# Eight experts' weights held on chip and addressed by a register, in two expert blocks of an eight-block network

## The reference

```
# block index 3
flat = (x - mean) * rsqrt(var + 1e-5) * ln_scale + ln_bias
h_shared = swiglu(flat @ shared_in_w.T);  out_shared = h_shared @ shared_out_w.T + shared_out_b
h_expert = swiglu(flat @ expert_in_w.T)                       # 512 wide, the same for all experts
routed = cnt @ expert_out_bias + sum_e comb[:, e] * (h_expert @ expert_out_weight[e].T)   # two e per token
# block index 7
h = relu(xf @ W1[e] + b1[e]);  y = h @ W2[e] + b2[e]          # 256 -> 256 -> 256, e = 0..7
y = (y - mean(y)) / sqrt(var(y) + 1e-5) * gamma[e] + beta[e]
out = sum over the token's two experts of gate * y
```

## Time and profile before

| | us |
|---|---|
| three timed runs | 3156.28, 3156.52 (median), 3159.9 |
| the profiled execution's own time | 3158.89 |
| its span, first to last instruction | 3157.1 |
| norm, block 3 (1090.3 to 1101.3) | 11.0 |
| parameter wait and second norm (to 1115.3) | 14.0 |
| routing (to 1136.8) | 21.5 |
| plan (to 1159.6) | 22.8 |
| gated layers `srh` (to 1249.9) | 90.3 |
| shared and routed output `sro` (to 1381.2) | 131.3 |
| norm, block 7 (2965.3 to 2977.1) | 11.8 |
| routing (to 2996.6) | 19.5 |
| plan (to 3020.4) | 23.8 |
| experts `nee` (to about 3143) | 122.4 |

### The profile page before, as it was taken

How to read it: one execution, slowest core, us unless ns; L and a number is a source line. 1 busy time by engine, 2 the same in 40 slices (tenths; PEclk the granted TensorE clock), 3 DMA queues, 4 the chain that set the end, 5 groups by cost and what they waited for, 6 DMA issues and landing times. The chain is left out here.

```text
span 3157.1 us, 52623 instructions
## 1 busy us (share of the span) xinstructions
PE 2438.4 (77%) x18539; PEld 2039.5 (65%) x18539; DVE 1574.7 (50%) x3095; ACT 1142.8 (36%) x2211; POOL 553.1 (18%) x862
## 2 busy tenths in 40 slices
PE   6979599679957758855785999998989999844255
PEld 4858499579936634644784777777777777734153
DVE  3646412222236631143445677777677777732355
ACT  2333122012213211122213666656566656614421
POOL 0000122122212100420001111212112211120044
PEclk8999699789969969976897999999999999967587
DMA  4000022134231102720565231324244452021075
GB/s 124 1 7 1 26 84 90 63 96 143 75 96 64 35 27 87 243 81 22 220 266 155 74 105 35 91 87 130 66 136 128 115 142 64 18 57 38 8 230 190
DMA packets 147048, 293.48 MB, mean 93 GB/s; under 512 B 37154, under 2 KB 74056, under 8 KB 143716
## 3 DMA queue, kind: packets, MB, share of 16 engines
q1 hardware_dynamic: 127988, 237.43, 24.3%
q0 software_dynamic: 18800, 52.69, 6.1%
HBM read 488.56 MB, written 65.74 MB: 176 GB/s over the span
## 5 line engine op out<-in xcount | busy, mean ns | idle before, releaser
L2224 PE MATMUL tx_ring<-g_ident,tx_p 128*128 128x128 f32 x2552 | 394.6, 283 | 74.1 <-DVE tx_p_t L2464 35.8
L2224 PEld LDWEIGHTS tx_ring<-g_ident,tx_p 128*128 128x128 f32 x2552 | 286.2, 141 | 176.8 <-DVE tx_p_t L2464 58.6
L2464 DVE COPY tx_p_t<-tx_ring 128x512 f32<-128x512 f32 x464 | 305.6, 685 | 132.3 <-PE tx_ring L2224 129.7
L2457 DVE TENSOR_REDUCE tx_neg_max<-tx_scores 128x1 f32<-128x1354 f32 x232 | 362.0, 1561 | 16.1 <-PE tx_scores L2212 16.1
L2354 ACT ACTIVATE tx_p<-tx_scores,tx_neg_max 128x1354 f32<-128x1354 f32 x232 | 322.9, 1392 | 87.3 <-DVE tx_neg_max L2457 84.7
L2361 ACT ACTIVATE tx_p_t<-tx_ring 128x384 f32<-128x384 f32 x232 | 113.7, 490 | 294.8 <-PE tx_ring L2224 290.9
L2212 PE MATMUL tx_scores<-tx_keys,tx_queries 96*128 96x512 f32 (+1 forms) x696 | 202.2, 399 | 16.3 <-DMA tx_queries<-tx_q_hi 11.2
L2264 PE MATMUL tx_ring<-tx_p_t,tx_values 128*32 128x128 f32 x5104 | 174.2, 298 | 14.7 <-ACT tx_p_t L2361 12.8
L2264 PEld LDWEIGHTS tx_ring<-tx_p_t,tx_values 128*32 128x32 f32 x5104 | 156.3, 121 | 28.2 <-ACT tx_p_t L2361 24.0
L192 PE MATMUL ln_turned<-g_ident,g_xn 128*128 128x128 f32 x176 | 39.5, 409 | 138.3 <-DVE g_xn L179 138.3
L2212 PEld LDWEIGHTS tx_scores<-tx_keys,tx_queries 96*128 96x128 f32 x696 | 115.3, 193 | 27.5 <-issue 17.1
(11 more groups left out here) (910 smaller groups left out, 5265.2 us busy)
## 6 DMA issues: line engine op xcount, KB each, us to landing
tx_keys<-expert_keys SPq DMA_DIRECT2D x696, 169.5 KB
lv1e_w<-in_L_ffn_W SPq DMA_DIRECT2D x232, 256.0 KB
tx_w<-in_L_ffn_W SPq DMA_DIRECT2D x58, 1024.0 KB
lv0e_w<-in_L_ffn_W SPq DMA_DIRECT2D x200, 256.0 KB
tx_values<-expert_values SPq DMA_DIRECT2D x58, 704.0 KB
tx_rows<-in_L_ffn_rows SPq DMA_DIRECT2D x29, 640.0 KB, 3.7
sro_we<-_L_ffn_expert_out_weight SPq DMA_DIRECT2D x29, 512.0 KB, 5.5
nee_w<-in_L_ffn_w SPq DMA_DIRECT2D x58, 256.0 KB, 4.1
```

What stands on the lines that cost most here:

```text
L2224: last = nc.tensor.transpose(ring[u % 2][:, (t - t0) * P:(t - t0 + 1) * P], p[n % 2][:, t * P:(t + 1) * P], g.ident[:])
L2457: nc.vector.tensor_reduce(neg_max[:, n % 4:n % 4 + 1], sc[n % 2][:, 0:N], AX_X, ALU.max, negate=True)\
L2464: nc.vector.tensor_copy(p_t[:, n % TURNED, t0:t0 + nt, :], ring[u % 2][:, 0:nt * P].rearrange("p (t q) -> p t q", q=P))\
```

## The change

Both blocks get a class that owns all of the block's weights for its whole length: `RoutedWeights` (8 expert matrices of 512 KB, two of 1 MB, one of 512 KB, the gates, their bias and the norm's parameters: 14 DMAs, 6.8 MB) and `NormedWeights` (`w1`, `w2`, the two broadcast rows of each expert, 256 KB each, and its bias columns, 1 KB, with the gate: 33 DMAs, 6.3 MB). SP issues them all in the block's first stage, the norm. The stages after it load no weights any more. For each tile the engines that use the weights now read the owner themselves (`owners`) and put the register into the operand's address: PE in `sro`; PE, ACT and DVE in `nee`. The stationary `w1` of `nee` isn't addressed that way: ACT copies the tile's `w1` (128x512) into one of two buffers `w1_now` (`bring`), and PE waits for it.

```diff
-def stage_route(nc, g, tag, src_t, gate, width, rule, weights, mask, bias=None, keys=None):
+def stage_route(nc, g, tag, src_t, gate, width, rule, weights, mask, keys=None, held=None):
 
     with ExitStack() as ctx:
         s = Pool(nc, ctx, tag)
-        w = s.sb("w", [P, KD, width])
+        w, w_loaded, bias_all = held or (s.sb("w", [P, KD, width]), s.sem("w_loaded"), None)
...
+            if held is None:
+                sync.dma_start(w[:], gate.rearrange("(k p) e -> p k e", p=P)).then_inc(w_loaded, 16)
...
-def stage_gated_hidden(nc, g, tag, src_t, shared_dram, expert_dram, h):
+def stage_gated_hidden(nc, g, tag, src_t, held, h):
...
-            for i, dram in enumerate((shared_dram, expert_dram)):
-                sync.dma_start(w[i][:], dram.rearrange("(k p) o -> p k o", p=P)).then_inc(w_loaded[i], 16)
...
         def _(sync):
-            owner = {}
-
-            def expert(i):
-                if i not in owner:
-                    owner[i] = nc.sync.value_load(plan.owner[0:1, i:i + 1], min_val=0, max_val=plan.experts - 1)
-                return owner[i]
-
-            def load(i):
-                k = i % ROUTED_SETS
-                new = dict(cond=expert(i) != expert(i - ROUTED_SETS)) if i >= ROUTED_SETS else {}
-                sync.dma_start(we[:, k, :, :].rearrange("p k o -> p (k o)"),
-                               expert_dram[bass.ds(expert(i), 1)].rearrange("o p n -> p (o n)"), **new).then_inc(we_loaded[k], 16)
-
-            sync.dma_start(ws[:], shared_dram.rearrange("(k p) o -> p k o", p=P)).then_inc(ws_loaded, 16)
-            for i in range(ROUTED_SETS):
-                load(i)
             back.load_table(sync)
-            for i in range(ROUTED_SETS, tiles):
-                sync.wait_ge(done, i - ROUTED_SETS + 1)
-                load(i)
             back.load(sync, sent, all_sent)
...
+            of = owners(nc.tensor, plan)
...
-                pe.wait_ge(we_loaded[i % ROUTED_SETS], 16 * (i // ROUTED_SETS + 1))
+                if i == 0:
+                    pe.wait_ge(we_loaded, 16 * plan.experts)
...
-                    last = nc.tensor.matmul(row[i % 2][:, 0:D], hg_t[:, i % 2, f, :], we[:, i % ROUTED_SETS, f, :],
+                    last = nc.tensor.matmul(row[i % 2][:, 0:D], hg_t[:, i % 2, f, :], we[:, of(i), f, :].rearrange("p o n -> p (o n)"),
...
+    def load(self, sync):
+        a = self.a
+        sync.dma_start(self.affine[:], a["L1_ffn_affine"]).then_inc(self.affine_loaded, 16)
+        sync.dma_start(self.gates[:], a["L1_ffn_gates"].rearrange("(k p) e -> p k e", p=P)).then_inc(self.gates_loaded, 16)
+        sync.dma_start(self.gate_bias[:], a["L1_ffn_gate_bias"].partition_broadcast(P)).then_inc(self.gates_loaded, 16)
+        for i, name in enumerate(("L1_ffn_shared_in_w", "L1_ffn_expert_in_w")):
+            sync.dma_start(self.w_in[i][:], a[name].rearrange("(k p) o -> p k o", p=P)).then_inc(self.w_in_loaded[i], 16)
+        sync.dma_start(self.ws[:], a["L1_ffn_shared_out_w"].rearrange("(k p) o -> p k o", p=P)).then_inc(self.ws_loaded, 16)
+        for e in range(self.experts):
+            sync.dma_start(self.we[:, e, :, :].rearrange("p k o -> p (k o)"), a["L1_ffn_expert_out_weight"][e])\
+                .then_inc(self.we_loaded, 16)
...
-                    sync.dma_start(affine[:], a["L1_ffn_affine"]).then_inc(loaded, 16)
-                    sync.wait_ge(loaded, 16)
+                    sync.wait_ge(held.affine_loaded, 16)
...
+def owners(eng, plan):
+
+    held = {}
+
+    def of(i):
+        if i not in held:
+            held[i] = eng.value_load(plan.owner[0:1, i:i + 1], min_val=0, max_val=plan.experts - 1)
+        return bass.ds(held[i], 1)
+    return of
...
+    def load(self, sync):
+        a = self.a
+        sync.dma_start(self.gate[:], a["L3_ffn_Wg"].rearrange("(k p) e -> p k e", p=P)).then_inc(self.gate_loaded, 16)
+        for e in range(self.experts):
+            sync.dma_start(self.w1[:, e, :, :].rearrange("p k o -> p (k o)"), a["L3_ffn_w"][e, :, 0:KD * D])\
+                .then_inc(self.w_loaded, 16)
+            sync.dma_start(self.w2[:, e, :, :].rearrange("p k o -> p (k o)"), a["L3_ffn_w"][e, :, KD * D:2 * KD * D])\
+                .then_inc(self.w_loaded, 16)
+            sync.dma_start(self.b1[:, e, :], a["L3_ffn_cols"][e]).then_inc(self.small_loaded, 16)
+            sync.dma_start(self.rows[:, e, :, :].rearrange("p r d -> p (r d)"),
+                           a["L3_ffn_rows"][e:e + 1].rearrange("o r d -> o (r d)").to_broadcast([P, 2 * D]))\
+                .then_inc(self.small_loaded, 16)
...
+        w1_now = s.sb("w1_now", [P, 2, KD, D])
...
-            for i in range(SETS):
-                load(i)
             back.load_table(sync)
-            for i in range(SETS, tiles):
-                sync.wait_ge(second_done, i - SETS + 1)
-                sync.wait_ge(out_done, i - SETS + 1)
-                load(i)
...
-                pe.wait_ge(w_loaded[i % SETS], 32 * (i // SETS + 1))
+                pe.wait_ge(brought, i + 1)
...
-                    last = nc.tensor.matmul(row[i % 2][:, 0:D], h[:, i % 2, f, :], w2[:, i % SETS, f, :],
+                    last = nc.tensor.matmul(row[i % 2][:, 0:D], h[:, i % 2, f, :], w2[:, of(i), f, :].rearrange("p o n -> p (o n)"),
...
+            def bring(i):
+                if i == 0:
+                    act.wait_ge(w_loaded, 32 * experts)
+                if i >= 2:
+                    act.wait_ge(first_done, i - 1)
+                nc.scalar.activation(w1_now[:, i % 2, :, :].rearrange("p k o -> p (k o)"),
+                                     w1[:, of(i), :, :].rearrange("p e k o -> p (e k o)"), ACT.Copy).then_inc(brought, 1)
...
-                                                bias=b1[:, i % SETS, f:f + 1])
+                                                bias=b1[:, of(i), f:f + 1].rearrange("p o c -> p (o c)"))
...
+                    bring(i + 2)
...
+                nc.vector.tensor_tensor(y[:, i % 3, :], row[i % 2][:, 0:D], rows[:, of(i), 0, :].rearrange("p o d -> p (o d)"), ALU.add).then_inc(y_done, 1)
...
+                nc.vector.tensor_tensor(out[:, i % 2, :], z[:, i % 2, :], rows[:, of(i), 1, :].rearrange("p o d -> p (o d)"), ALU.mult).then_inc(out_done, 1)
...
+                if i == 3:
+                    sr_weights = RoutedWeights(nc, Pool(nc, inner, "srw"), a)
+                    early = sr_weights.load
+                if i == 7:
+                    ne_weights = NormedWeights(nc, Pool(nc, inner, "new"), a)
+                    early = ne_weights.load
```

110 lines of the change are left out of this document (54 added, 56 removed).

## The result

The changed kernel takes **3124.1 us** (3122.4 to 3124.8) against 3156.4 (3155.4 to 3159.9) of the kernel before: a ratio of **0.9895**, interval 0.9878 to 0.9912. That is 32.3 us less; the forecast was 36.8 less, 3119.7, with a range of 3109 to 3137. The profiled execution went from 3158.9 to 3124.6, 34.3 less.

The account below looks back on a forecast made before the run. Bounds: load waits at stage heads, landing of sends in `sro`, SP's issuing in `nee`. -14.7 - 11.4 - 11.4 + 3.8 - 3.1 = -36.8 us takes the profiled 3158.9 to 3122.1; from the median 3156.5, 3119.7, range 3109 to 3137.

Parts of the forecast that it names:

- Part 1: Heads of block 3's stages: waits for loads at parameters, routing, gated layers and shared product go, barriers stay; -14.7 us.
- Part 2: Loop of `sro`: weights leave the DMA queues, sends land sooner, POOL's own order decides; 80.4 to 69.0 us, -11.4.
- The cover for PE's read: In `sro`, PE's 0.7 us register read runs while the array still works, plus 0.4 us slack a tile; priced at nothing.
- Part 3: Loop of `nee`: SP's 3.25 us of issuing goes, a chain with register reads sets 2.7 a tile; last send -11.4 us.
- R: Time one register read adds on PE, ACT or DVE; taken as 0.7 us, bounds 0.45 and 1.1.
- The chain: In `nee`, dependent steps over two tiles, lengthened by register reads and the `w1` copy from 3.33 to 5.3 us.
- Part 4: Issuing moved into the norms: block 3 nothing, block 7's barrier 3.8 us late, its routing's gate wait gone, -3.1 us.
- 1 (the array waits): The array waits with the sequencer for the register; `sro` stays at 2.87 a tile, 3131 us; chance 0.11.
- 2 (R of 1.1): A register read costs 1.1 us, so `nee` gives only 1 us; 3130 us; chance 0.11.
- 3 (sends land as late): In `sro`, POOL's own gathers held the sends, not the weights; gain there near 0, 3131 us; chance 0.08.
- 4 (SP held by the bytes): The queue holds SP in both norms until the bytes finish; +12 in block 3, +6 more in block 7; 3138; chance 0.09.
- 5 (slower): Register reads stand bare on every engine and cost well over their row on SP; +15 us, 3172; chance 0.05.

Follow-up runs that it names:

- e8: The change, but block 3's routing gate weights and bias are loaded at the stage's head as before; 3154.2 us, ratio 0.9961, 5.0 over the change.
- e4: The change with block 7's loads in 11 DMAs instead of 33, same bytes; 3141.8 us, 7.3 under the change.
- e3: The change without the choice of expert: constant weight addresses, so no register reads in either loop; 3136.3 us, 12.9 under the change.
- e2: The change with PE, ACT and DVE reading the expert's number ahead of the tile's waits; 3142.3 us, ratio 0.9921, against the change's 3149.2.
- e7: The change, with SP also loading 512 KB of unused expert weights per tile in `sro`; 3151.8 us, ratio 0.9954, 2.6 over the change.
- e12: The change with reads ahead of the waits and block 7's loads in 11 DMAs; 3105.8 us against 3158.6 of the kernel before, ratio 0.9833.

## Why the prediction was right, and where its terms were off

The mechanisms were the ones that the traces show, and three of four parts came out within about 1 us of the forecast. That the sum lies within 4.4 us of the median is luck in part. The loop of `nee` gave 4.9 us in place of 10.3, the way to the first send of `sro` and the barrier of block 7 cost 2.0 more than forecast, and against that stand 2.2 us of clock that I had not priced and 2.3 of scatter between two executions. It was luck too that the first measurement fell on ground A: on ground B the same change gives 17 us, and the forecast of 37 would have been wrong there.

The stages of the two first traces, by the starts of their first instructions:

| term | forecast | trace |
|---|---|---|
| parameter wait | -1.6 | -1.3 |
| routing, block 3: start | -3.0 | -3.1 |
| routing, block 3: products faster | not seen | -2.2 |
| gated layers | -6.3 | -6.4 |
| shared product | -3.8 | -4.2 |
| `sro` ahead of its first send | 0 | +1.1 |
| `sro` loop | -11.4 | -12.2 |
| between `sro` and block 7 | 0 | -2.3 (scatter) |
| block 7: barrier and gate | +0.7 | +1.6 |
| block 7: routing and plan | 0 | -0.2 |
| `nee` ahead of its first send | -1.1 | -0.7 |
| `nee` loop | -10.3 | -4.9 |

The trace's terms add up to -34.6, and the two profiled executions differ by 34.3.

**Part 1** held. Its miss is the 2.2 us of the clock: I read the waits as time and not as what they do to the products behind them. The row was there to be read. In the kernel before, the 44 products of routing ran at the lower level in both blocks:

```profile
1118.40:1128.20 9.80, 9.56 (x44) 9.46 (x44) 0.12 (x1) 0.00 (x0) 0.00 (x0) 0.50 0.00 1
2980.40:2990.00 9.60, 9.55 (x44) 9.46 (x44) 0.00 (x0) 0.00 (x0) 0.00 (x0) 0.50 0.00 0
```

`e8` undoes one wait and the clock with it, `e4` takes one away in block 7 and gains it.

**Part 2** held in size on ground A: 2.57 a step until the gathers end. One sign that I had named did not show: DVE was to wait for no send over 1 us, and it waits 18 times, up to 2.8 us. The sign was wrong and not the mechanism. A send lands about 2.6 us after its issue (1282.33, and DVE's copy that waited for it starts at 1284.96), well within the 4.4 that the loop allows, and DVE, which has little to do, is idle until then. The cover for PE's read held as well (`e3`), but only inside the loop: ahead of the first send nothing covers it, and that costs 0.9 of the 1.1 us (5.0 against 4.1 in `e2`, where the read lies ahead of the wait). That the weights' bytes made the sends land late is supported by the gathers' landing, 5.7 us before and 3.4 after, and only weakly by `e7`; no run on ground A puts the bytes back alone.

**Part 3** is the term that was mis-sized. R was right at 0.7. The chain was forecast at 5.3 for two tiles and is 5.7: copy to ReLU took 1.06 where 0.85 had been put down (0.26, 0.49 for the copy of `w1` and 0.1 for the register instruction). From the rows' copy to the copy of `w1` it took 0.52 us, since the first now runs to its end (0.36) and 0.16 of idle time follow; from the copy of `w1` to the ReLU it took 0.54, close to the 0.49 of the earlier trace rows. Second product to `nee_y` took 1.90 in place of 1.76. I took 5.3 / 2 = 2.66 and rounded to 2.7; 5.7 / 2 = 2.85, and 2.90 was measured as the mean of steps that vary, behind the first, from 2.57 to 3.42 until the gathers end. The 0.2 a step are 5.5 of the 28 steps' us. That the reads behind the waits held the loop is shown by `e12`, where they stand ahead of them: 2.58. Its other edit is in the norm's loads, which have landed long before this loop.

**Part 4.** The barrier came 16.3 us after SP's start, 15.5 was forecast; PE started 16.7 us after the norm's beginning, 15.0 before. The products behind it stayed at the lower clock (0.50), since the idle time had only changed its cause, from 4.08 to 5.72 us.

**The rivals.** 1 (the array waits): no, by the step of 2.57 and by `e3`. 2 (R of 1.1): no, the loads' median is 0.28 to 0.31. 3 (sends land as late): no on ground A. 4 (SP held by the bytes): no; with the same bytes in 11 pieces (`e4`) routing starts 4.7 us earlier. 5 (slower): its mechanism, bare reads on every engine, was near none of the traces; but on ground B block 7's half gives nothing or a small loss, and the same kernel without the reads is 12.9 us faster, a cost that no rival named.

## What to carry to other kernels

A register read costs 0.7 us where it stands behind a wait that is on the critical chain, and nothing ahead of that wait if the engine idles there; written one line earlier, the reads of this loop cost 8.7 us less (on ground A). On an engine whose row is full it stays in the row. When loads are moved into an earlier stage, count the pieces that the issuing engine must send before that stage's barrier, and merge them until they fit under the stage's own work. A wait ahead of a run of small products can cost more than its length: here 44 products took 9.56 us behind a wait of 4.1 and 7.34 behind one of 1.0. And a change in a tile loop should be measured on more than one chip: this one gave 32 us on one and 17 on another.
